# A rewritten timetable for a two-layer block: two part tiles, and transposes in front of scores

## The reference

```python
x = x + _L0_xattn_ref(_layernorm(x), ctx_1024, ctx_1024, mask, W, b)         # A: masked attention
x = x + _L0_ffn_ref(_layernorm(x), weight)                                   # Hadamard, 4-bit rounding, ternary product
x = x + _L1_xattn_ref(_layernorm(x), ctx_1024, fside, Wq, ..., W1, b1, W2, b2, ...)  # C: attention with a bias, then gelu(..W1)W2
x = x + _L1_ffn_ref(_layernorm(x), Wr, W1, b1, W2, b2)                       # 8 experts, each takes its best 512 tokens
```

## Time and profile before

| | us |
|---|---|
| three runs, median (lowest to highest) | 1018.82 (1014.47 to 1024.16) |
| the profiled execution | 1022.7 |
| its span, first to last instruction | 1020.9 |
| mean granted TensorE clock | 0.884 |

### The profile page before, as it was taken

How to read it: one execution, slowest core, us unless ns; L and a number is a source line. 1 busy time by engine, 2 the same in 40 slices (tenths; PEclk the granted TensorE clock), 3 DMA queues, 4 the chain that set the end, 5 groups by cost and what they waited for, 6 DMA issues and landing times. The chain is left out here.

```text
span 1020.9 us, 19107 instructions
## 1 busy us (share of the span) xinstructions
PE 777.3 (76%) x6121; PEld 671.6 (66%) x6121; DVE 663.9 (65%) x2038; ACT 615.2 (60%) x1274; POOL 441.3 (43%) x619
## 2 busy tenths in 40 slices
PE   0677787788797788877878797787823299999995
PEld 0566566677676677666767686676612189999985
DVE  2777877957974886687487578664157566666441
ACT  0666766777677678667657766775110066666662
POOL 5524425415533452452344135123230347777752
PEclk9987978999899989979898897988965599999998
DMA  5946837737645653753546565710041025555541
GB/s 152 264 117 146 257 76 195 193 84 183 164 108 134 158 161 84 182 174 84 141 118 171 130 166 145 195 54 21 11 143 52 22 71 147 142 133 129 134 73 22
DMA packets 95680, 131.10 MB, mean 128 GB/s; under 512 B 7648, under 2 KB 88032, under 8 KB 91488
## 3 DMA queue, kind: packets, MB, share of 16 engines
q1 hardware_dynamic: 89440, 121.52, 43.7%
q0 software_dynamic: 6144, 8.39, 4.6%
HBM read 104.72 MB, written 25.17 MB: 127 GB/s over the span
## 5 line engine op out<-in xcount | busy, mean ns | idle before, releaser
L795 ACT ACTIVATE probs<-neg,neg_max 128x256 f32<-128x256 f32 x512 | 232.0, 504 | 79.8 <-DVE neg_max L606 79.6
L613 DVE TENSOR_TENSOR p_lo<-ps_t,p_hi 128x512 f16<-128x512 f32 x256 | 176.4, 689 | 56.6 <-ACT p_hi L802 56.5
L802 ACT ACTIVATE p_hi<-ps_t 128x512 f16<-128x512 f32 x256 | 151.0, 590 | 74.3 <-PE ps_t L356 73.3
L356 PE MATMUL ps_t<-ident,probs 128*128 128x128 f32 x1024 | 173.2, 296 | 22.2 <-ACT probs L795 21.9
L356 PEld LDWEIGHTS ps_t<-ident,probs 128*128 128x128 f32 x1024 | 137.5, 153 | 61.7 <-ACT probs L795 35.7
L348 PE MATMUL ps_s<-k_diag,q_stack 128*128 128x512 f32 x256 | 150.0, 587 | 27.8 <-DMA q_stack<-q_dram 18.9
L606 DVE CUSTOM_DVE_ANT_0 neg<-ps_s,bias 128x256 f32<-128x256 f32 x256 | 97.7, 419 | 73.5 <-issue 45.9
L606 DVE CUSTOM_DVE_ANT_0 neg<-ps_s,mask_add 128x256 f32<-128x256 f32 x224 | 85.0, 417 | 35.7 <-PE ps_s L348 22.3
L1063 POOL TENSOR_TENSOR o_sum<-o_raw 128x128 f32<-128x128 f32 x64 | 30.0, 469 | 168.9 <-ACT o_raw L927 168.4
L377 PE MATMUL ps_o<-v_parts,p_hi 128*128 128x49 bf16 x1024 | 92.3, 190 | 0.0
L377 PE MATMUL ps_o<-v_parts,p_lo 128*128 128x49 bf16 x1024 | 90.5, 188 | 0.0
(11 more groups left out here) (245 smaller groups left out, 1791.3 us busy)
## 6 DMA issues: line engine op xcount, KB each, us to landing
bias<-in_bias SPq DMA_DIRECT2D x64, 512.0 KB, 4.5
k_diag<-k_dram SPq DMA_DIRECT2D x64, 256.0 KB, 4.6
q_stack<-q_dram SPq DMA_DIRECT2D x32, 512.0 KB, 6.6
k_dram<-part SPq DMA_DIRECT2D x64, 128.0 KB, 3.0
q_dram<-part SPq DMA_DIRECT2D x64, 128.0 KB, 2.4
w1e<-in_w1e SPq DMA_DIRECT2D x8, 1024.0 KB, 4.9
w2e<-in_w2e SPq DMA_DIRECT2D x8, 1024.0 KB, 6.6
ctxT_A<-in_ctxT SPq DMA_DIRECT2D x8, 256.0 KB, 7.3
```

Source lines behind the costliest of these rows:

```text
L356: ins = nc.tensor.matmul(ps_t[g % 2][:, (j * QT + kb) * P:(j * QT + kb + 1) * P], probs[:, g % 2, j, kb * P:(kb + 1) * P], ident[:, :], st ...
L613: nc.vector.tensor_tensor(p_lo[:, g % 3, :], ps_t[g % 2][:, :], p_hi[:, g % 3, :], ALU.subtract).then_inc(lo_ready, 1)
L795: ins = nc.scalar.activation(probs[:, g % 2, j, :], neg[:, g % 3, j, :], ACT.Exp, bias=neg_max[:, g % 3, j:j + 1], scale=-1.0)
L802: nc.scalar.activation(p_hi[:, g % 3, :], ps_t[g % 2][:, :], ACT.Copy).then_inc(hi_ready, 1)
```

## The change

- All slots come from one table, `timetable()`. For most batches the k and v products move from slot 0 to slot 4 of the C segment two before, the C normalisation and its q into the same segment (slots 3 and 10 to 13); the A normalisation three segments ahead and its q and k two ahead; the Hadamard, rounding and ternary steps of A from the C segment into the A segment behind it (slots 0 to 9); the gelu from slot 0 to slot 3, the first product's pieces to slots 11 to 15 and 0 to 2, the second's to 7 to 14; G, R and the logits into later segments. The last batches have slots of their own.
- There are two `part` tiles, used in turn, with a semaphore each.
- In each slot TensorE transposes the probabilities of unit g in front of the scores of unit g+2.
- Helpers get other banks; on each engine the helpers of one slot come in another order; the gelu of the last two batches is counted by quarters; SyncE's list is written out by slot, and stacks that are ready a segment early are loaded at its start.

```diff
+def timetable():
+    t = {}
+
+    def put(b, seg, **slots):
+        for job, s in slots.items():
+            t[job, b] = (seg, s) if isinstance(s, int) else s
+
+    for p in range(NB):
+        i = POS[A, p]
+        if p == 0:
+            put(p, -1, ka=0, ln_a=1, nrm_a=2, qa=3, x_bias=15, v_a=3, mask=8)
+        elif p <= 2:
+            put(p, i - 1, ln_a=0, nrm_a=1, x_bias=2, qa=3, ka=6, v_a=3, mask=8)
+        elif p == 3:
+            put(p, i - 2, ln_a=8, nrm_a=9, x_bias=10, qa=10, ka=12)
+            put(p, i - 1, mask=7, v_a=10)
+        else:
+            put(p, i - 3, ln_a=3, nrm_a=3, x_bias=11)
+            put(p, i - 2, qa=1, ka=8)
+            put(p, i - 1, mask=7, v_a=10)
+    for c in range(NB):
+        i = POS[C, c]
+        if c == 0:
+            put(c, i - 2, v=1, k=1, k_low=2, v_copy=2)
+            put(c, i - 1, ln_c=2, nrm_c=3, xc=5, q0=6, q1=7, qc=8, v_c=9)
+        elif c == LAST - 1:
+            put(c, i - 2, v=1, v_copy=2, k=2, k_low=3)
+            put(c, i - 1, ln_c=3, nrm_c=3, xc=6, q0=7, q1=7, qc=8, v_c=8)
+        elif c == LAST:
+            put(c, i - 2, v=4, k=4, k_low=5, v_copy=5)
+            put(c, i - 1, ln_c=5, nrm_c=7, xc=8, q0=9, q1=10, qc=10, v_c=6)
+        else:
+            put(c, i - 2, v=4, k=4, k_low=5, v_copy=5, ln_c=3, nrm_c=3, xc=10, q0=11, q1=12, qc=13)
+            put(c, i - 1, v_c=11)
+    for r in range(NB):
+        i = POS[A, r] + 1
+        if r < 2:
+            put(r, i, oa=4, wa0=5, wa1=6, x1=7, nrm_b=8, hb=9, had0=10, had1=11, amax=12, cap=13, qi=14, tern=15, yq=15)
+            put(r, i + 1, x2=0)
+        elif r == LAST:
+            put(r, i, oa=6, wa0=7, wa1=8, x1=9, nrm_b=11, hb=12, had0=13, had1=14, amax=15)
+            put(r, i + 1, cap=1, qi=2, tern=3, yq=4, x2=4)
+        else:
+            put(r, i, oa=6, wa0=7, wa1=8, x1=9, nrm_b=11, hb=14)
+            put(r, i + 1, had0=0, had1=1, amax=2, cap=5, qi=5, tern=6, yq=8, x2=9)
+    for f in range(NB):
+        i = POS[C, f] + 1
+        if f == LAST:
+            put(f, i, oc=3, wo0=4, wo1=4, y=5, nrm_f=6, z=6, y_bias=7, gelu0=8, gelu1=8)
+            put(f, i + 1, yf=1, nrm_g=2, affine=2, x3=3, ln_r=4, nrm_r=5, xr=6, logits=6, copy=7)
+        elif f == LAST - 1:
+            put(f, i, oc=6, wo0=7, wo1=8, y=9, nrm_f=11, z=12, y_bias=13)
+            put(f, i + 1, gelu0=2, gelu1=4, yf=9, nrm_g=9, affine=10, x3=10, ln_r=11, nrm_r=11, xr=12, logits=13, copy=14)
+        else:
+            put(f, i, oc=4, wo0=5, wo1=6, y=7, nrm_f=9, z=10, y_bias=10, raw0=13, raw1=15)
+            put(f, i + 1, gelu0=3, gelu1=3)
+            put(f, i + 2, yf=0, nrm_g=4 if f < LAST - 2 else 1, affine=4 if f < LAST - 2 else 2, x3=6 if f < LAST - 2 else 3)
+            if f < LAST - 3:
+                put(f, i + 3, ln_r=3, nrm_r=3)
+                if f < LAST - 4:
+                    put(f, i + 4, xr=9, logits=10, copy=11)
+                else:
+                    put(f, i + 4, xr=5, logits=6, copy=7)
+            elif f == LAST - 3:
+                put(f, i + 3, ln_r=3, nrm_r=3, xr=13, logits=14, copy=15)
+            else:
+                put(f, i + 2, ln_r=7, nrm_r=8, xr=9, logits=9, copy=12)
+    return t
+
+
+AT = timetable()
+DUE = {(job, *at): b for (job, b), at in AT.items()}
+
+
+def due(job, i, s):
+
+    return DUE.get((job, i, s))
+
+
+def ff1_pieces(f):
+
+    i = POS[C, f] + 1
+    if f == LAST:
+        return {(i, 7): tuple(range(FC))}
+    if f == LAST - 1:
+        return {(i + 1, 0): tuple(range(FC))}
+    return {(i + (11 + n) // UNITS, (11 + n) % UNITS): (n,) for n in range(FC)}
+
+
+def ff2_pieces(f):
+
+    i = POS[C, f] + 2
+    if f == LAST:
+        return {(i, 0): tuple(range(8))}
+    if f == LAST - 1:
+        return {(i, 5): (0, 1, 2, 3), (i, 8): (4, 5, 6, 7)}
+    if f == LAST - 3:
+        return {(i, 9 + n): (n,) if n < 6 else (6, 7) for n in range(7)}
+    return {(i, 7 + n): (n,) for n in range(8)}
+
+
+FF1_DUE = {at: (f, pieces) for f in range(NB) for at, pieces in ff1_pieces(f).items()}
+FF2_DUE = {at: (f, pieces) for f in range(NB) for at, pieces in ff2_pieces(f).items()}
+FF1_BANKS = [("m0", "m1", "m0", "m1") if f < LAST - 1 else ("s0", "s1", "t0", "t1") for f in range(NB)]
+FF2_BANK = ["m0"] * (LAST - 2) + ["m1", "m1", "m0"]
+IN_PSUM = [(2, 3) if f < LAST - 1 else (0, 1, 2, 3) for f in range(NB)]
...
-def prep_c_slots(i):
-    if i in FF2 and i in REST_A:
-        return dict(stats=1, apply=2, T=3, q=(4, 5), parts=5, values=4, bank="m0")
-    return dict(stats=2, apply=3, T=5, q=(6, 7), parts=7, values=4, bank="m0" if i in REST_A else "m1")
...
-def rest_a_slots(i):
-    return dict(oT=4, out=(5, 6), x1=7, apply=8, T=9, had=(10, 11), amax=12, cap=13, qT=14, tern=15)
...
-def ff1_slots(i):
-    if i in FF2 and i < NSEG:
-        pieces = {11: (0, 1), 12: (2, 3), 13: (4,), 14: (5,), 15: (6, 7)}
-        raw = (12, 13)
-    elif i >= NSEG:
-        pieces, raw = {9: tuple(range(FC))}, ()
-    else:
-        pieces = {9: (0, 1), 10: (2,), 11: (3,), 12: (4,), 13: (5,), 14: (6,), 15: (7,)}
-        raw = (10, 12)
-    return dict(oT=3, out=(4, 5), y=6, apply=7, T=8, bias=8, pieces=pieces, raw=raw, bank="s1" if i >= NSEG else "m0",
-                banks=("t0", "t1", "s1", "m0") if i >= NSEG else ("m1", "m0", "m1", "m0"))
-
-
-def ff2_slots(i):
-    bank = "m1" if i in FF1 else "m0"
-    if i == NSEG + 1:
-        return dict(gelu=0, pieces={1: tuple(range(8))}, y=2, apply=3, x3=4, bank=bank)
-    if i == NSEG:
-        return dict(gelu=3, pieces={6: (0, 1, 2, 3), 10: (4, 5, 6, 7)}, y=11, apply=12, x3=13, bank=bank)
-    if i in PREP_C:
-        return dict(gelu=0, pieces={6: (0, 1), 7: (2, 3), 8: (4, 5), 9: (6, 7)}, y=10, apply=11, x3=12, bank=bank)
-    return dict(gelu=0, pieces={2 + n: (n,) for n in range(8)}, y=10, apply=11, x3=12, bank=bank)
-
-
-def ff3_slots(i):
-    return dict(stats=0, apply=1, T=2, logits=3, copy=3, bank="s0" if i >= NSEG else "m1")
...
+        K_BANK = ["m0" if c == LAST - 1 else "m1" for c in range(NB)]
+        QA_BANK = ["m1" if p < 3 else "m0" for p in range(NB)]
+        QC_BANK = ["m0" if c in (0, LAST - 1) else "m1" for c in range(NB)]
+        R_BANK = ["m1"] * (LAST - 3) + ["m0", "o0", "o0", "o0"]
...
         def pe_layers(pe):
-            for i in range(-1, NSEG + 3):
+            for i in range(-1, NSEG + 2):
                 for s in range(UNITS):
                     g = i * UNITS + s
+                    if 0 <= g < NUNIT:
+                        pe_prob_transposes(pe, g)
                     if 0 <= g + 2 < NUNIT:
                         pe_scores(pe, g + 2)
-                    if 0 <= g < NUNIT:
-                        pe_prob_transposes(pe, g)
                     if 0 <= g - 2 < NUNIT:
                         pe_values(pe, g - 2)
                     pe_kv(pe, i, s)
-                    pe_ff3(pe, i, s)
                     pe_prep_a(pe, i, s)
+                    pe_rest_a(pe, i, s)
                     pe_prep_c(pe, i, s)
-                    pe_rest_a(pe, i, s)
                     pe_ff1(pe, i, s)
                     pe_ff2(pe, i, s)
+                    pe_ff3(pe, i, s)
                     pe_start(pe, i, s)
...
         def ac_part_high(ac, n, src, scale):
-            wait(ac, S["part_out"], 64 * n)
-            nc.scalar.activation(part_flat(0), src, ACT.Copy, scale=scale).then_inc(S["part_h"], 1)
+            wait(ac, S[f"part_out{n % 2}"], 64 * (n // 2))
+            nc.scalar.activation(part_flat(n, 0), src, ACT.Copy, scale=scale).then_inc(S["part_h"], 1)
...
         def ve_layers(ve):
-            for i in range(-1, NSEG + 3):
+            for i in range(-1, NSEG + 2):
...
                     ve_kv(ve, i, s)
-                    ve_ff3(ve, i, s)
-                    ve_prep_a(ve, i, s)
-                    ve_prep_c(ve, i, s)
+                    ve_ff2(ve, i, s)
+                    ve_norm_stats(ve, i, s)
+                    ve_norm_apply(ve, i, s)
+                    ve_prep_a_low(ve, i, s)
                     ve_rest_a(ve, i, s)
+                    ve_prep_c_low(ve, i, s)
                     ve_ff1(ve, i, s)
-                    ve_ff2(ve, i, s)
+                    ve_logits(ve, i, s)
...
+        def sp_stacks_early(sp, i):
+
+            kind, b = SEGMENTS[i + 1] if i + 1 < NSEG else (None, None)
+            if kind is not None and AT["ka" if kind == A else "k", b][0] < i:
+                sp_k_in(sp, kind, b)
+            if kind is not None and AT["qa" if kind == A else "qc", b][0] < i:
+                sp_q_in(sp, kind, b)
+
+        def sp_stacks(sp, i, s):
+            c = due("k_low", i, s)
+            if c is not None:
+                sp_part_out(sp, C, c, "k")
+            p = due("qa", i, s)
+            if p is not None:
+                sp_part_out(sp, A, p, "q")
+                if POS[A, p] == i + 1:
+                    sp_q_in(sp, A, p)
+            p = due("ka", i, s)
+            if p is not None:
+                sp_part_out(sp, A, p, "k")
+                if POS[A, p] == i + 1:
```

(48 more changed lines are left out.)

566 lines of the change are left out of this document (251 added, 315 removed).

## The result

The changed kernel takes 1011.81 us (median of 20 runs, 1006.98 to 1015.13), the kernel before 1019.18 beside it (20 runs, 1011.43 to 1027.26). The ratio is 0.9924, with a 95% interval of 0.9901 to 0.9948: 7.7 us less. The forecast was 1017 with a range of 994 to 1036. The profiled execution has a span of 1012.5 us and takes 1014.3; against the one before that is 8.4 us less, so the two can be laid side by side, stage by stage.

The account below looks back on a forecast made before the run. No engine is always busy; hand-overs between engines set the pace. Profiled 1022.7 + 2 (first segments) - 18 (pairs) + 2 (last segments) + 12.5 (tail) = 1021.2; less 3.9, about 1017 us, range 994 to 1036.

Parts of the forecast that it names:

- The tail: After the last attention units: batch 7's second product queues behind batch 6's transposes and logits; +12.5 us, from 9 to 15.
- The pairs: Four regular pairs of C and A segments: each gains 4.5 us, between 0 and 8; 18 us in all.
- ScalarE's wait for k and its copy: In the gelu's stretch of each pair: this wait and copy go, about 2.0 of 7.86 us.
- The exchange of the normalisations: VectorE in the pairs: normalisations go under the gelu, Hadamard and rounding steps take their slots; nothing taken, 3 us upper end.
- The wait behind the low part: TensorE in each pair: 2.7 us falls to about 1.0, as the second part tile removes ScalarE's wait.
- R "goes": TensorE's wait for the normalised R, 2.0 us per pair, goes because several slots now lie between.
- F "stays": TensorE's wait for F, 1.95 us per pair, stays, being one slot apart as before.
- The swap: Transposes in front of scores in each slot: 0.5 us lost per pair, between 2.0 lost and as much gained.
- The last segments: Last three segments: C5 gains 3 us, TensorE waits 5 for the last q's stack; sum +2, from -4 to +8.
- The pairs pack better: Rival, chance 0.22: VectorE's idle time under the gelu makes pairs fall towards 80 us; 991 to 1005.
- Slower: Rival, chance 0.24: swap costs 2.0 us per pair, `qi` wait grows to about 4, pairs gain 1 or less; 1033.
- The tail is no loss: Rival, chance 0.07: batch 6's rows come earlier or the last product is late anyway; 1006 us.

Follow-up runs that it names:

- tail_b6: Changed kernel with batch 6's router transposes, logits and their copy queued behind batch 7's second product on TensorE; 1001.63 us, ratio 0.9813 to the kernel before.
- k_in_gelu: Changed kernel with the regular batches' k and v products in the gelu's slot 3 instead of slot 4; 1024.59 us, ratio 1.0018 to the kernel before.
- norms_late: Changed kernel with the regular pairs' A, C and R normalisations moved from the gelu's slot 3 to slots 7 and 8; 1030.26 us, ratio 1.0078.
- before_two: Kernel before the change with two part tiles and nothing else of the change; 1003.58 us, ratio 0.9811 to the kernel before.
- q_early: Changed kernel with the last segment's q two slots earlier and batch 3's router transposes, logits and copy in slots 9 to 11; 1005.37 us, ratio 0.9839.
- best: Changed kernel with batch 5's and 6's logits out of the last product's way, cap and yq earlier, last segment's q two slots earlier; 977.56 us, ratio 0.9557.

## Why the prediction was right, and where its terms were not

It said that the pairs would gain about what the tail loses, and they did; 1011.8 is 5 us below 1017. In the profile the gap is 6.9 us (1014.3 against 1021.2): pairs 4.8, last segments 2.5, opening and first segments 2.1 better than said, the tail 2.3 and the experts 0.2 worse.

*The tail*, the term with the most weight, was right in its mechanism and its place: `tail_b6` takes one entry out of the product's way and gets 11 us back. It was short by two sizes. The product was costed at its old 8.86 us "by the rule and by the row"; behind the wait of 6.32 it took 9.95, in a window with a granted clock of 0.72 where it had 0.81. So more of it ran at 1.2 GHz than before. The Trainium skill ("TensorE: Matmul & The Clock Gate", "HAM oscillation — how this bites in real kernels") says that an idle TensorE falls to half its clock and has to earn it back; the trace agrees, and the forecast had read the rule and kept the old length. And batch 6's first product in the head cost 1.8, not 1: its y comes 30.2 us into the tail instead of 28.4 (706.52 on VectorE, against 728.12). One sign came out otherwise: the gap in front of batch 6's transposes was to be some 11 us and is 6.32, because batch 5's logits, with a wait of 3.25 of their own, stand in the same stretch. The delay of the product is there all the same.

*The pairs*: -18 against -22.8, but the terms do not add up to it one by one; several were sized wrongly, in both directions.
- ScalarE's wait for k and its copy: 2.0 taken, and the gelu's stretch of C3 is 2.1 shorter (5.76 against 7.86). This term was right. The 3.4 of `k_in_gelu` are the price of k's place in the new slot, where the wait is longer.
- The exchange of the normalisations for the Hadamard and rounding steps: nothing taken, 3 as the upper end. No run exchanges the two alone; `norms_late` puts the normalisations' place under the gelu at 3.3 per pair on average, and at 5.3 in C2 and C3. The prediction counted three of them in every pair; C1 and C4 hold two.
- The wait behind the low part: the text gave it to the second tile. In the pairs the slots do it, the tile adds nothing there. And removing it was taken at 1.7 of 2.7 us; on the old timetable, in the profile of `before_two`, the tile alone shortens a pair by 4.5. Of this 2.5 lie in the C segment, where the wait stood (slots 3 and 4 of C3 fall from 3.9 and 4.0 us to 1.9 and 2.4). The other 2.0 lie in the A segment behind it, where ScalarE never waited for the tile and the granted clock was 0.91 to 1.00 instead of 0.87 to 0.91; whether the tile gave them or the chance of this one execution stays open.
- R "goes": it came back as a wait for the bank, 1.9 us per pair. F "stays": it fell to 0.35. The rounded activations stay, as said, at 3.75; 0.9 of it is the longer `q_int`, which the forecast had not seen.
- The transposes' wait for the exponentials, 1.05 per pair before and 5.0 after, was not in the sum at all.
- Nor was the clock. TensorE's busy time in the pairs fell by 13.5 us, of which fewer instructions explain 1.8 (15 of 2304). The rest goes with the higher clock, which is argued. A sum over waits alone can't see this part.

*The swap*: 0.5 per pair was taken between -2 and +2; on the new timetable it is 0.1. That holds for this change. As a rule for the edit it fails: on the old timetable it costs 13 us, outside the +8 named for it in that run.

*The last segments*: the stall of the stack, 5 between 2 and 6.5, was 6.67. Not foreseen was that batch 3's logits hold bank m1 for 3.0 us in front of the rows from which q is made. C5 gained 8.1 (50.0 to 41.9) instead of 3, which covers it.

*The rivals.* "The pairs pack better" had a true mechanism and not the size: 81.8 us per pair, a gain of 5.7 where 7 was given as the point. "Slower" had the wait for the rounded activations right (3.75, about 4 said), but the swap did not take 2.0 per pair. "The tail is no loss" fell. One sum behind the range is off: measured from the forecast, the bounds of the parts add up to -29.5 and +32.5, not -29 and +30; nothing hangs on it.

## What to carry to other kernels

When helpers move between slots, read each engine's queue in its new order and ask of each entry what stands directly behind it that was ready earlier: here one group of transposes in front of the last large product cost 11 us, half of what the pairs had won. Give a step and its consumer on another engine two slots, not one and not none: here consumers in the same slot waited 3.75 us and one slot behind 2.6 (the router's transposes) and 3.3 (C's rows in `q_early`), while two slots removed the first two waits; F, one slot apart, waited only 0.35. Test each part of a large change alone: here a second buffer, the smallest part, was by itself worth more than the whole.

## What the runs showed of the hardware

The same matmuls of the last product, 32 of them, took 9.95, 8.84 and 7.14 us: behind a wait of 6.32 us and two short steps, behind one of 3.25 and a short step, and behind work with a wait of 0.23. The granted clock of the three stretches was 0.72, 0.81 and 1.00: at 2.4 GHz throughout the last, at 1.2 GHz for part of the other two. The same shows over whole segments: C3 after the change, with no wait of TensorE above 1.62 us, was granted 1.00, A6 behind it, with one of 3.81, only 0.84. That removing such a wait also shortens the matmuls behind it is argued from these rows, as no run changed the clock alone. And the waits do not settle the clock: C6 of `q_early` and of `best`, with the same matmuls and nearly the same waits, were granted 0.92 and 0.81, and TensorE was busy 30.07 and 33.80 us. A gain read from one execution of a segment can be off by such an amount, here 2.9 us of 41.5.

VectorE's `q_int`, from float32 to bf16, 128x512, took 1.37 us each time that POOL's 1.32 us addition on nrm_G ran beside it, 0.54 where other POOL work ended 0.26 us into it, and 0.43 with no POOL work beside it. No run moved POOL's work alone, so that it is the cause is argued.
